# Routing weights brought to the partitions by DMA instead of by TensorE, in a four-unit audio block

## The reference, cut to what matters

```
x: (8, 256, 128)
h = token_mixer(x)                    # three 128x128 products, log-space scan over time: 257 positions
h = h + attention(layernorm(h))       # 8 heads of 16; sequence b reads keys and values of b+4
n = layernorm(h)                      # "xn" below
logits = n @ gate_w + gate_b          # 16 experts
w, idx = top_k(softmax(logits), 2);  w = w / sum(w)
cw = sum(one_hot(idx) * w)            # (rows, 16): the routing weights, two of 16 not zero
for each of 16 experts, and one shared expert whose weight is 1:
    g = clip(n @ w1_gate + b, -cg, cg)
    v = clip(n @ w1_up   + b, -cu, cu)
    t = g * sigmoid(alpha * g) * scale * (v + shift)       # 96 hidden features
    y += cw[expert] * (t @ w2 + b2)
return h + y
```

## Time and profile before

| | |
|---|---|
| median of three runs | 359.9 us |
| the profiled execution | 359.87 us |
| its span, first to last instruction | 358.1 us |
| PE busy | 319.3 us (89%), 2352 matmuls |
| ACT busy | 261.7 us (73%) |
| DVE busy | 257.7 us (72%) |
| POOL busy | 116.1 us (32%) |
| chain that ended last | PE 65%, DVE 14%, ACT 11% |
| mean granted TensorE clock | 0.953 |

### The profile page before, as it was taken

One profiled execution on the slowest core, in us unless ns is written; L12 is line 12 of the kernel. 1 busy time (PEld: TensorE's weight loads), 2 busy tenths in 40 slices (PEclk: granted clock), 3 DMA queues, 4 the chain that ended last, 5 costly groups with the idle time before them and its releaser, 6 DMA issues.

```text
span 358.1 us, 6481 instructions
## 1 busy us (share of the span) xinstructions
PE 319.3 (89%) x2352; PEld 235.9 (66%) x2352; DVE 257.7 (72%) x506; ACT 261.7 (73%) x432; POOL 116.1 (32%) x89
## 2 busy tenths in 40 slices
PE   3245999968999999999899999999999999998993
PEld 1013555546767767867476777887768768998972
DVE  2495792117989576988958596978868757899991
ACT  3968714669886878899558888994876869488731
POOL 2003810010741512640521733450033143424571
PEclk9765899998999999999969999999999999999998
DMA  7600000000000000000000000001000000000000
GB/s 255 278 0 0 29 3 3 0 2 29 2 0 2 3 1 2 0 3 0 0 2 3 1 2 2 0 29 31 3 3 0 0 2 2 1 2 29 3 0 29
DMA packets 3518, 6.75 MB, mean 19 GB/s; under 512 B 280, under 2 KB 2464, under 8 KB 3360
## 3 DMA queue, kind: packets, MB, share of 16 engines
q1 hardware_dynamic: 3488, 6.35, 4.9%
HBM read 5.29 MB, written 1.05 MB: 18 GB/s over the span
## 4 chain that ended last, share of the span: by engine, by line
PE 65%; DVE 14%; ACT 11%; issue 4%; POOL 3%; DMA 1%; POOLq 0%; SPq 0%; ACTq 0%; DVEq 0%
PE slot L894 65%; DVE mx L721 3%; DVE gbuf L809 2%; DVE ubuf L815 1%; POOL te L450 1%; DMA cst<-in_consts 1%; DVE ubuf L829 1%; DVE tbuf L821 1%; ACT osb L640 1%; DVE w1l L873 1%; ACT zabs L479 1%; ACT soft L480 1%; ACT w1h L518 1%; ACT L467 1%; POOL soft L397 1%
## 5 line engine op out<-in xcount | busy, mean ns | idle before, releaser
L450 POOL TENSOR_TENSOR te<-tbuf,ubuf 128x516 f32<-128x516 f32 x52 | 76.7, 1484 | 129.2 <-DVE ubuf L829 108.6
L894 PE MATMUL slot<-xh,w1h 128*128 128x258 f32 x208 | 65.5, 315 | 1.2 <-DVE h L841 0.4
L894 PE MATMUL slot<-xl,w1h 128*128 128x258 f32 x208 | 59.3, 285 | 0.0
L894 PE MATMUL slot<-xh,w1l 128*128 128x258 f32 x208 | 59.2, 285 | 0.0
L721 DVE TENSOR_REDUCE mx<-slot 128x2 f32<-128x514 f32 x64 | 40.8, 687 | 11.6 <-PE slot L894 11.4
L894 PE MATMUL slot<-te,w 128*128 128x258 f32 x208 | 48.3, 383 | 0.7 <-POOL te L450 0.6
L617 ACT ACTIVATE gbuf<-slot,cst 128x516 f32<-128x516 f32 x52 | 35.6, 690 | 17.0 <-PE slot L894 16.3
L894 PEld LDWEIGHTS slot<-xh,w1h 128*128 128x128 f32 x208 | 40.2, 193 | 11.3 <-issue 10.3
L624 ACT ACTIVATE ubuf<-slot,fpar 128x516 f32<-128x516 f32 x52 | 35.5, 688 | 16.6 <-PE slot L894 15.3
L829 DVE TENSOR_TENSOR ubuf<-slot,ubuf 128x516 f32<-128x516 f32 x52 | 35.9, 692 | 16.0 <-PE slot L894 15.1
L576 ACT ACTIVATE pt<-slot 128x516 f32<-128x516 f32 x64 | 35.1, 600 | 14.9 <-PE slot L894 14.6
(11 more groups left out here) (150 smaller groups left out, 531.1 us busy)
## 6 DMA issues: line engine op xcount, KB each, us to landing
pt<-in_w SPq DMA_DIRECT2D x1, 1664.0 KB, 9.2
xt<-in_x SPq DMA_DIRECT2D x4, 256.0 KB, 3.2
out<-osb SPq DMA_DIRECT2D x8, 128.0 KB
te<-in_sel SPq DMA_DIRECT2D x1, 832.0 KB, 10.7
w<-in_w SPq DMA_DIRECT2D x1, 832.0 KB, 12.3
cst<-in_consts SPq DMA_DIRECT2D x1, 624.5 KB, 5.6
cst<-in_consts SPq DMA_DIRECT2D x1, 193.5 KB, 4.5
out<-osb SPq DMA_DIRECT2D x8, 0.5 KB
```

What stands on the lines that cost most here:

```text
L450: g.tensor_tensor(te[:, c % NTE, :, :], tbuf[:, c % NB, :, :], ubuf[:, c % NB, :, :], ALU.mult)\
L894: return nc.tensor.matmul(out_, lhsT, rhs, start=start, stop=stop, **k)
```

## The change

The routing weights no longer pass through TensorE. A new piece `rows` stores the 17 partitions of `cwt` to a scratch tensor `spill` in DRAM. A new piece `spread` reads it back for each of the chunks 0 to 11: two DMAs a chunk, each copying one expert's row to the 32, 64 or 96 partitions that belong to it, into `cwb`, a ring of NSP = 4 chunks. POOL multiplies `tbuf` by `cwb`. The matrix `sel`, its load, its rounding, its 104 matmuls and the PSUM uses "cw" are gone. Chunk 12, the shared expert, needs no weight: DVE forms its `te` itself, and POOL has 12 products a unit instead of 13.

The up half of chunks 0 to 11 no longer passes through ACT: DVE clips it straight out of PSUM (bounds shifted by the bias), and a new DVE operation `gu` adds the bias and multiplies it into `tbuf` in one instruction. Only chunk 12 keeps the old way. The routing on DVE loses two small operations.

The last query position's maximum takes one fp32 matmul instead of two; for that ACT writes a third copy of k (`kw`) per unit. The rounding of the first-layer weights is cut into four parts on ACT and four on DVE. TensorE gets 24 pieces `warm`, each with two products of a zero tile with itself into a PSUM slot, in the waits of its first unit. The tables AT and SLOT are new throughout. The title of the change speaks of the gate clip on VectorE; it is there before as well.

```diff
 NB = 4
 NTE = 8
+NSP = 4
...
+WPARTS = 4
+NWARM = 24
+WPART = 2 * NF * P // WPARTS
+SHARED = NF - 1
...
-    "g": "PA", "clip_gate": "V", "tanh": "A", "gated": "V", "u": "PA", "clip_up": "V", "cw": "PV",
-    "te": "G", "down": "P", "add": "V", "out": "PA", "store": "S",
+    "g": "PA", "clip_gate": "V", "tanh": "A", "gated": "V", "u": "PA", "clip_up": "V", "gu": "V",
+    "rows": "S", "spread": "S", "te": "G", "down": "P", "add": "V", "out": "PA", "store": "S",
...
+    if name == "u" and engine == "A":
+        return numbers[0] == SHARED
...
-        t += [("T", n, u) for n in ("weights", "low", "clamps", "parameters")]
+        t = [("T", "warm", u, k) for k in range(NWARM)] + t
+        t += [("T", n, u, k) for k in range(WPARTS) for n in ("weights", "low")]
+        t += [("T", n, u) for n in ("clamps", "parameters")]
...
-    a += [("A", "route", u, k) for k in range(ROUTE)] + [("A", n, u) for n in ("split", "cwt", "keep")]
+    a += [("A", "route", u, k) for k in range(ROUTE)] + [("A", n, u) for n in ("split", "cwt", "rows", "keep")]
...
-        f += [("F", n, u, c) for n in ("g", "clip_gate", "tanh", "gated", "u", "clip_up", "cw")]
-        f += [("F", "te", u, c)]
+        f += [("F", n, u, c) for n in ("g", "clip_gate", "tanh", "gated", "u", "clip_up", "gu")]
+        if c < SHARED:
+            f += [("F", "spread", u, c), ("F", "te", u, c)]
...
 AT = {
     "P": (
-        0, 2, 3, 5, 4, 6, 11, 7, 8, 10, 12, 14, 17, 18, 19, 23, 21, 20, 22, 24, 26, 27, 9, 15, 13, 16, 25, 29, 30, 28,
+        10, 30, 7, 18, 1, 14, 6, 17, 13, 59, 46, 11, 16, 3, 71, 15, 19, 62, 2, 24, 22, 25, 4, 5, 0, 9, 12, 23, 21, 20,
...
-        sel = sb("sel", [P, NF, P], F32R)
+        zeros = sb("zeros", [P, P])
+        kw = sb("kw", [P, 2, 2, W])
+        cwb = sb("cwb", [P, NSP, 2, W])
...
-            sp.dma_start(sel_stage, sel_in).then_inc(s_sel, 16)
...
+            def rows(st, u):
+                released(sp, At(uses, "A", u), ("cwt",))
+                sp.dma_start(spill[u], cwt[0:NE, :, :]).then_inc(s_rows, 16)
+
+            def spread(st, u, c):
+                sp.wait_ge(s_rows, 16 * (u + 1))
+                b = c % NSP
+                ge(sp, "te", SHARED * u + c + 1 - NSP)
+                for e in range(P * c // I, (P * c + P - 1) // I + 1):
+                    begin, end = max(P * c, I * e) - P * c, min(P * c + P, I * e + I) - P * c
+                    sp.dma_start(cwb[begin:end, b, :, :], spill[u, e:e + 1].to_broadcast([end - begin, 2, W]))\
+                      .then_inc(s_spread[b], 16)
...
             def te_(st, u, c):
-                ge(pool, "gg", NF * u + c + 1)
-                released(pool, st, ("cw", c))
+                ge(pool, "gu", SHARED * u + c + 1)
+                pool.wait_ge(s_spread[c % NSP], 32 * ((SHARED * u + c) // NSP + 1))
...
-                g.tensor_tensor(te[:, c % NTE, :, :], tbuf[:, c % NB, :, :], ubuf[:, c % NB, :, :], ALU.mult)\
+                g.tensor_tensor(te[:, c % NTE, :, :], tbuf[:, c % NB, :, :], cwb[:, c % NSP, :, :], ALU.mult)\
                     .then_inc(S["te"], 1)
...
-            def weights(st, u):
+            def weights(st, u, k):
+                at = slice(WPART * k, WPART * k + WPART)
                 act.wait_ge(s_w1, 16)
-                a(w1h[:, :, :, :].rearrange("p k c n -> p (k c n)"), w1_stage, ACT.Copy).then_inc(s_high, 1)
-                act.wait_ge(s_sel, 16)
-                a(sel[:, :, :].rearrange("p c n -> p (c n)"), sel_stage, ACT.Copy).then_inc(s_high, 1)
+                a(w1h[:, :, :, :].rearrange("p k c n -> p (k c n)")[:, at], w1_stage[:, at], ACT.Copy).then_inc(s_high, 1)
...
-            def masked(st, u, name, tile, **k):
+            def masked(st, u, name, tile, whole=None, **k):
...
+                if whole is not None:
+                    a(whole[:, u % 2, :, :], src, ACT.Copy)
...
-                    done(v.tensor_tensor(cw[:, :, 0:E], cw[:, :, 0:E], cw2[:, :, :], ALU.add))
-                    after(17)
-
-                    done(v.tensor_copy(cwp[:, :, 0:NE].bitcast(F32R), cw[:, :, :]))
-                    after(18)
-                    done(v.tensor_tensor(cwp[:, :, 32:32 + NE], cw[:, :, :], cwp[:, :, 0:NE], ALU.subtract))
+                    done(v.tensor_tensor(cwp[:, :, 0:E], cwp[:, :, 0:E], cw2[:, :, :], ALU.add))
...
             def clip_up(st, u, c):
-                released(dve, st, ("u", c))
                 p = c % NB
-                v.tensor_scalar(ubuf[:, p, :, :], ubuf[:, p, :, :], fpar[:, UHI, c:c + 1], fpar[:, ULO, c:c + 1],
-                                ALU.min, ALU.max).then_inc(S["uclip"], 1)
+                hi, lo = fpar[:, UHI, c:c + 1], fpar[:, ULO, c:c + 1]
+                if c == SHARED:
+                    released(dve, st, ("u", c))
+                    v.tensor_scalar(ubuf[:, p, :, :], ubuf[:, p, :, :], hi, lo, ALU.min, ALU.max).then_inc(S["uclip"], 1)
+                else:
+                    filled(dve, st, ("u", c))
+                    gu_before(dve, u, c)
+                    release(v.tensor_scalar(ubuf[:, p, :, :], slot(st, ("u", c))[:, :, 0:W], hi, lo, ALU.min, ALU.max),
+                            st, ("u", c))
...
-            def cw_(st, u, c):
+            def gu(st, u, c):
 
                 p = c % NB
-                filled(dve, st, ("cw", c))
-                ge(dve, "uclip", NF * u + c + 1)
-                release(v.tensor_tensor(ubuf[:, p, :, :], slot(st, ("cw", c))[:, :, 0:W], ubuf[:, p, :, :], ALU.mult),
-                        st, ("cw", c))
+                ge(dve, "gg", NF * u + c + 1)
+                if c == SHARED:
+                    ge(dve, "uclip", u + 1)
+                    filled(dve, st, ("down", 1))
+                    v.tensor_tensor(te[:, c % NTE, :, :], ubuf[:, p, :, :], tbuf[:, p, :, :], ALU.mult)\
+                        .then_inc(S["shared"], 1)
+                else:
+                    released(dve, st, ("u", c))
+                    v.scalar_tensor_tensor(tbuf[:, p, :, :], ubuf[:, p, :, :], fpar[:, UB, c:c + 1], tbuf[:, p, :, :],
+                                           ALU.add, ALU.mult).then_inc(S["gu"], 1)
...
-            def low_weights(st, u):
-                dve.wait_ge(s_high, 1)
-                then(v.tensor_tensor(w1l[:, :, :, :].rearrange("p k c n -> p (k c n)"), w1_stage,
-                                     w1h[:, :, :, :].rearrange("p k c n -> p (k c n)").bitcast(F32), ALU.subtract))
+            def low_weights(st, u, k):
+                at = slice(WPART * k, WPART * k + WPART)
+                dve.wait_ge(s_high, k + 1)
...
+            def warm(st, u, k):
+
+                name = ("warm", k)
+                take(pe, st, name)
+                if k == 0:
+                    pe.wait_ge(s_blank, 1)
+                fill(mm(slot(st, name)[:, 0, 0:P], zeros[:, :], zeros[:, :]), st, name)
+                release(mm(slot(st, name)[:, 1, 0:P], zeros[:, :], zeros[:, :]), st, name)
...
-                for i in range(2):
-                    mm(slot(st, name)[:, 0, 0:W], bq[:, i, s, :], ka[:, u % 2, i, 1 - s, :], start=(i == 0), stop=(i == 1))
+                released(pe, At(uses, "T", u), ("k",))
+                mm(slot(st, name)[:, 0, 0:W], bq[:, s, :], kw[:, u % 2, 1 - s, :])
...
-            def cw_(st, u, c):
-
-                name = ("cw", c)
-                take(pe, st, name)
-                released(pe, At(uses, "A", u), ("cwt",))
-                if u == 0:
-                    pe.wait_ge(s_high, 2)
-                for s in range(2):
-                    last = mm(slot(st, name)[:, s, 0:W], sel[:, c, :], cwt[:, s, :])
-                fill(last, st, name)
-
...
                 for c in range(begin, end):
-                    ge(pe, "te", NF * u + c + 1)
+                    if c == SHARED:
+                        ge(pe, "shared", u + 1)
+                    else:
+                        ge(pe, "te", SHARED * u + c + 1)
```

115 lines of the change are left out of this document (68 added, 47 removed), and 112 rows, old and new, of tables (AT, ENGINES, SLOT).

## The result

The changed kernel takes 339.89 us (median of four runs, 339.33 to 341.7) against 359.93 us; the ratio is 0.9458, with a 95% interval of 0.9417 to 0.9499. The prediction was 341 us, 332 to 353. The profiled execution has a span of 338.1 us, 20.0 less than before. The total is right; of the terms behind it several are not, and two errors of some 5 us each cancel.

What follows compares the result with a forecast made beforehand. It took TensorE to bound the middle (98 to 316 us), VectorE the last unit's experts, and no single engine the start. Sum: 359.9 - 3.5 (start) - 15 (middle) - 0 (end) = 341.4, forecast 341 us, range 332 to 353.

Steps and rivals of the forecast that it cites:

- The low weights: Start, 0 to 98 us: three of four low parts now follow the mixer's result h, 2.7 us less.
- The zero products: Start: they fit TensorE's idle time and may keep the clock high; 2 us lost to 1.4 won, taken as 0.7 gained.
- Start, 3.5 us in sum: 0 to 98 us: low weights 2.7, L684 0.9, kw -1.4, mlast 0.6, zero products 0.7; 3.5 us less.
- This stretch is TensorE's: Middle, 98 to 316 us: TensorE sets it; sel 14.6 and mlast 2.2 off, 1.8 given back, 15 us less.
- ScalarE's relief: Middle: ACT loses 36 up copies, gets two kw copies, 171.3 to 147.9 us busy; it has room, no gain counted.
- The clip out of PSUM: Middle: DVE's clip taken at 692 ns like L829, 36 x 39 ns = 1.4 us more VectorE work.
- Middle, DVE 174.7 busy of 201: Middle: VectorE gets 3.8 us more, 87% of the shortened stretch; its 14.9 us of waits for sel lose their cause.
- End, taken as 0: 316 to 358 us: VectorE's pace, 3.1 us more against 1.2, 0.5 and 1.5 less; sum 0.1, taken as 0.
- more won: Rival, 332 us, chance 0.19: middle gains 19.0 + 2.7 and 3 us of waits for slots and ACT, start 3.5.
- exposed spread: Rival, 366 us, chance 0.08: last unit's four-chunk ring waits on DMA landings, binding above 6.2 us a landing.
- VectorE takes the middle: Rival, 348 us, chance 0.18: VectorE's 32.2 us other idle stays, clip costs 5.5 us; middle only 7 us shorter.
- no gain: Rival, 359 us, chance 0.05: TensorE was not the limit; start and middle both keep their length.

Runs made afterwards that it cites:

- e2: Changed kernel with the four roundings and four low parts of the first-layer weights put together again ahead of unit 0's h: 343.85 us, ratio 0.9574.
- e1: Changed kernel without its 48 zero products on TensorE (NWARM = 0): 342.22 us, ratio 0.9529.
- e3: Changed kernel with one more fp32r product per sequence in the up half of each chunk of units 0 to 2, 39 pairs: 346.83 us, ratio 0.9669.
- e9: Kernel before without its 104 sel products, their slots and waits; a second SBUF clip stands in L829's place: 358.18 us, ratio 0.9968.
- e10: Changed kernel with the gate half of units 0 to 2 copied out of PSUM twice by ScalarE, 39 more operations: 354.28 us, ratio 0.9852.
- e5: Kernel before without its 104 sel products, their slots and waits; L829 multiplies by a constant SBUF tile instead: 358.74 us, ratio 1.0006.
- e4: Changed kernel with the gate clip of units 0 to 2 done twice by VectorE, 39 more operations: 355.31 us, ratio 0.9887.
- e11: Changed kernel with the routing weights stored to DRAM twice, one store behind the other's landing, before the spread: 342.12 us, ratio 0.9537.
- e7: Changed kernel with the up half of the last unit's twelve chunks clipped by ScalarE in two Relu passes instead of VectorE: 347.59 us, ratio 0.9691.
- e12: Changed kernel with the last unit's second add behind the shared chunk's product, and zero products before the last down burst and output transposes: 339.0 us, ratio 0.9439.

## Why the prediction was right, step by step

- **The low weights, 2.7 us: right.** e2 puts them at 3.3 us to the landmark.
- **The zero products, 0.7 us within -2 to +1.4: too small, and outside the range.** e1 puts them at 2.3 to 2.9 us. I priced one group of eight products at the lower level; in e1 the whole start runs at 0.86. What the zeros occupy costs nothing that shows.
- **Start, 3.5 us in sum: 4.7.** With the measured 3.3 and 2.9 in place of 2.7 and 0.7 the sum would be 6.3; what is missing, 1.6 us, lies in the terms of L684, `kw` and `mlast`, and no run separates these. One of them was also summed wrongly: two halves of `mlast` are four records of 0.27 us, 1.1 us, not 0.6.
- **"This stretch is TensorE's", 15 us: wrong as a premise for the kernel before, and too small in size (21.7).** TensorE was busy 18.6 us less, of which e3's price gives 8.4 to the `sel` products and the clock some 3.4: in the kernel before the granted clock is at half from 178.0 to 184.8 us, after the change it is full in the whole middle, and half of 6.8 us is 3.4. What ended this stretch is not isolated: e9 and e10 have one too, e5 has none. The other 6.8 us are put down to `mlast` and to what a separate pair adds between attention products, which e3, whose pairs stand inside an accumulation, doesn't have; this split is worked out, not isolated. TensorE's idle time fell by another 3.1 us.
- **ScalarE's relief counted at nothing ("It has room"): the step that failed.** e10 gives it 22.9 us back in the middle and it costs 13.5, 3.4 of them by the clock, with the reserve made there. The change took 22.6 us of it away in the middle. The prices of e3, e4 and e10 can't be summed: 8 and 13.5 us are together what was gained, though VectorE's dearer clip (below) had to be paid out of it. What they suggest is that three engines, at 99%, 87% and 76% in the changed kernel, hold one another.
- **The clip out of PSUM, 0.692 us: mis-sized, 0.809.** A clip with two pointer scalars out of PSUM is slower than L829's product out of PSUM. For 36 chunks that is 36 x (809 - 653) ns = 5.6 us against 1.4.
- **Middle, DVE 174.7 busy of 201: 173.5 of 198.4.** The two agree by luck. Between the landmarks VectorE was busy 173.0 us before, so it got only 0.5 us more, not 3.8. The operations of the chunks rose by 7.6 us (108.8 to 116.4), more than the 5.3 forecast, and all others fell by 7.1 us instead of 1.5: a small operation behind `mlast` runs half as often (L734 3.1 us, L776 1.4), two maxima less fall into the window (1.3 us), and one of the routing's takes 0.24 us where it took 0.57 (L768, L809).
- **End, taken as 0: wrong, 6.4 us lost.** VectorE is the pace there, as said; its operations were priced too low. I had 3.1 us more for it against 3.2 less. But 1.7 of these 3.2 us stand inside the routing, before the landmark; measured there, my sum says 1.6 us longer for the end and 16.7 shorter for the middle, against 6.4 and 21.7. From the routing's end to VectorE's last product of a chunk it takes 41.3 us instead of 33.3, 8.0 more where I had 3.1; from there to the last add 2.1 instead of 3.0, a gain of 0.9 where I had 1.5. By lines (288.9 to 338.1 after, 315.8 to 358.1 before) the up clips cost 2.0 us more, the two products 1.9, the gate clips 1.3, `gated` 1.3 and the add 0.7. TensorE, too, has more left to do behind the landmark (127 of the experts' records with `w1` instead of 111), so a small part of the middle's gain is work handed on. In the last 34 us before the tail the mean of L863 is 861 ns, of L877 858, of L857 802, where before L821 had 741, L829 688 and L815 707:

```profile
L877 DVE SCALAR_TENSOR_TENSOR tbuf<-ubuf,fpar,tbuf 128x516 f32<-128x516 f32 x12 | 10.1, 858 | 0.0
L863 DVE SCALAR_TENSOR_TENSOR tbuf<-tbuf,gbuf 128x516 f32<-128x516 f32 x11 | 9.4, 861 | 0.2
L845 DVE TENSOR_SCALAR gbuf<-gbuf,fpar 128x516 f32<-128x516 f32 x9 | 6.9, 770 | 0.6 <-ACT gbuf L662 0.6
L857 DVE TENSOR_SCALAR ubuf<-slot,fpar 128x516 f32<-128x516 f32 x8 | 6.4, 802 | 0.0
```
- **The rival "more won": its place was right (the middle), its total not,** since the end took 6.4 us back. The rival of an exposed spread is refuted: landings of 2.9 us against the 6.2 from which it was to bind, and e11 puts 2.9 us more at 2.2. The rival "VectorE takes the middle" named the dearer clip rightly (5.5 us), but TensorE stood still for 1.5 us only. The rival "no gain" fell, since both the start and the middle are shorter.
- **The signs.** `h` of unit 0 was ready at 23.85 us (25 forecast), DVE's 15.1 us of waits for PE before L829 became 7.9 us before the new clip, `spread` landed in 2.9 us; the new clip read 0.81 us and not 0.69, and four `te` waited for a DMA.
- **Luck.** The start was 1.2 us better than its sum, the middle 5.0 better and the end 4.8 worse. The total is within 2 us because the last two cancel, and nothing in the prediction ties them together.

The stretched operations have one row as witness. In after's last unit POOL's `te` and a clip in SBUF start together, and the clip takes 1.53 us where it took 0.55 a little earlier; a clip out of PSUM that runs wholly beside the next `te` takes its 0.80:

```profile
306.92 0.55 DVE L845 TENSOR_SCALAR gbuf<-gbuf,fpar 128x516 f32<-128x516 f32 x1 [0.61 <-ACT gbuf L662]
...
308.07 1.32 POOL L494 TENSOR_TENSOR te<-tbuf,cwb 128x516 f32<-128x516 f32 x1 [3.10 <-PE slot L949]
308.14 1.53 DVE L845 TENSOR_SCALAR gbuf<-gbuf,fpar 128x516 f32<-128x516 f32 x1
...
311.75 1.54 POOL L494 TENSOR_TENSOR te<-tbuf,cwb 128x516 f32<-128x516 f32 x1 [2.36 <-DVE tbuf L877]
...
312.05 0.80 DVE L857 TENSOR_SCALAR ubuf<-slot,fpar 128x516 f32<-128x516 f32 x1
```

The Trainium skill has this in "SBUF — State Buffer", section "Who interferes with whom": a VectorE operation with two SBUF inputs, or one in a two-port mode, shuts out a GpSimd operation that reads SBUF and is shut out by it, for the whole instruction. The trace agrees: L857 and L829, which read PSUM, never pass 818 and 698 ns, L877 with both inputs in SBUF reaches 1794, and e5 and e9 turned a 692 ns operation into one of 987 and 947 by moving its operand into SBUF. By this rule the change had a price that the prediction missed: L829 was a PSUM reader standing right before POOL's `te`, and its heir L877 reads SBUF twice. In the changed kernel the PSUM read moved to the clip.

## What to carry to other kernels

- An engine at 76% that stands between two products of the busiest one can be part of the bound. Before taking a stretch as one engine's, ask of every engine what the next piece waits for; put some load on each, one at a time, and read the slope, and look whether the granted clock moved with it (3.4 of e10's 13.5 us).
- Price a VectorE operation by what runs on GpSimd beside it in that place, not by its mean elsewhere: 0.55 us alone was 1.5 us beside a GpSimd product. The clip out of PSUM took half as much again as the one in SBUF alone (808 against 543 ns), and about half of it beside GpSimd's product (0.80 against 1.53 us).
- Shortening one in-order list by loading another pays only if nothing that the first one waits for is queued behind the new work (e7).

## What was not expected of the hardware

- A 128x516 clip by two per-partition scalars took 808 ns out of PSUM (800 to 818 in 48), where a product of a PSUM and an SBUF tile of that shape took 695.
- A DMA of 34 KB into DRAM landed in 2.88 us, and DMAs of 64 to 194 KB out of it, one row read by up to 96 partitions, in 2.9 us at the median (1.8 to 4.6); SyncE needed 0.30 us to issue one at the least and 0.43 at the median, so the issue of 96 of them is 41 us of its time.
- TensorE's zero products shorten the kernel by 2.3 us although they make it busier: at the start the granted clock rose from 0.86 to 0.94 with them, and in the tail (e12) from 0.67 to 0.88.
- The granted clock was at half for 6.8 us in the middle of the kernel before, of e9 and of e10, each time behind a few waits of TensorE of half a us (8.0 us with 6.5 busy before 178.0), and full throughout the middle of the changed kernel and of e5.
